# Attention sums from the value product itself, and another order of the second pass

## What is computed

```python
x = x + autocorrelation(layernorm(x), ctx, ctx)           # layer 0
x = x + lora_product(layernorm(x))
Q, K, V = layernorm(x) @ Wq + bq, ctx @ Wk + bk, ctx @ Wv + bv      # layer 1
scores = einsum('bhgqd,bhkd->bhgqk', Q, K) / sqrt(16)     # 8 key heads h, 4 query groups g
w = softmax(scores, axis=-1)
y = einsum('bhgqk,bhkd->bhgqd', w, V)
x = x + y @ Wo + bo
h = relu(layernorm(x) @ up_w) ** 2
shared = h @ down_w
routed = (layernorm(x) @ fc1 @ expert) * top2_sum(logits) @ fc2
x = x + layernorm(shared + routed, gamma, beta)
```

## Time and profile before

| | us |
|---|---|
| median of three runs | 686.14 (685.78 to 686.70) |
| profiled execution | 687.42 |
| its span | 685.6 |
| PE busy in the span | 654.6 (95%) |
| DVE, ACT, POOL busy | 511.4, 432.0, 378.5 |
| granted PE clock | 0.999 of 2.4 GHz |

### The profile page before, as it was taken

The page is one execution under the profiler, slowest core; times in us unless marked ns, Lnnn a source line. Parts: engine busy times, 40 slices in busy tenths (PEclk is TensorE's granted clock), DMA queues, the critical chain, the costliest instruction groups (busy, mean ns, idle before and its releaser), DMA issues.

```text
span 685.6 us, 12653 instructions
## 1 busy us (share of the span) xinstructions
PE 654.6 (95%) x3964; PEld 482.3 (70%) x3964; DVE 511.4 (75%) x1140; ACT 432.0 (63%) x793; POOL 378.5 (55%) x464
## 2 busy tenths in 40 slices
PE   7889999999999898999999999999999999998986
PEld 3455666666656476788778787887878878786775
DVE  4999998999975877777677677776777767775444
ACT  4788888888746785574655846658367474674221
POOL 1388999888775534435455354554454545535351
PEclk9999999999999999999999999999999999999999
DMA  8334434352126321121212312113021221211000
GB/s 269 121 109 124 139 123 124 123 180 98 62 94 173 117 79 33 46 64 61 63 35 57 90 33 61 45 49 90 31 61 54 69 61 31 61 31 47 17 16 31
DMA packets 32551, 54.37 MB, mean 79 GB/s; under 512 B 5344, under 2 KB 7136, under 8 KB 32512
## 3 DMA queue, kind: packets, MB, share of 16 engines
q1 hardware_dynamic: 32512, 53.90, 26.6%
HBM read 36.84 MB, written 8.39 MB: 66 GB/s over the span
## 4 chain that ended last, share of the span: by engine, by line
PE 78%; DVE 11%; issue 4%; DMA 3%; ACT 3%; POOL 1%; SPq 0%; POOLq 0%; DVEq 0%; ACTq 0%
PE ps_b L1295 8%; PE ps_b L1297 7%; PE ps_b L1296 7%; PE wide L1295 7%; PE wide L1297 6%; PE wide L1296 6%; PE ps_b L1496 4%; PE ps_a L1340 4%; PE bank L1432 3%; DMA ctx_t<-in_ctx 3%; PE wide L1422 3%; PE ps_b L1350 3%; PE ps_a L1295 2%; PE ps_a L1297 2%; PE wide L1550 2%
## 5 line engine op out<-in xcount | busy, mean ns | idle before, releaser
L780 POOL TENSOR_TENSOR va<-mv,small 128x1 f32<-128x1 f32 x80 | 15.3, 192 | 149.0 <-DVE mv L1274 79.5
L745 ACT ACTIVATE stage<-wide 128x512 f32<-128x512 f32 x30 | 16.3, 595 | 83.8 <-PE bank L1597 83.7
L868 POOL TENSOR_TENSOR y_l<-y,y_h 128x512 fp32r<-128x512 f32 x16 | 21.9, 1370 | 72.5 <-ACT y_h L653 72.5
L1142 DVE RECIPROCAL y<-ps_b 128x256 f32<-128x256 f32 x32 | 55.9, 1748 | 0.4 <-PE ps_b L1496 0.4
L676 ACT ACTIVATE probs<-wide 128x1024 f32<-128x1024 f32 x32 | 32.8, 1025 | 36.1 <-PE wide L1550 36.1
L1295 PE MATMUL wide<-up_h,t_h 128*128 128x512 f32 x128 | 52.1, 407 | 1.5 <-DVE t_l L1226 1.5
L1297 PE MATMUL wide<-up_h,t_l 128*128 128x512 f32 x128 | 50.9, 398 | 0.0
L1296 PE MATMUL wide<-up_l,t_h 128*128 128x512 f32 x128 | 50.4, 394 | 0.0
L1295 PE MATMUL ps_b<-down_h,ht_h 128*128 128x512 f32 x120 | 49.6, 413 | 0.4 <-DVE ht_l L1214 0.4
L782 POOL TENSOR_TENSOR rs<-va,small 128x1 f32<-128x1 f32 x80 | 44.5, 557 | 6.3
L1297 PE MATMUL ps_b<-down_h,ht_l 128*128 128x512 f32 x120 | 47.2, 393 | 0.0
(11 more groups left out here) (244 smaller groups left out, 2155.9 us busy)
## 6 DMA issues: line engine op xcount, KB each, us to landing
q_stack<-qt_h SPq DMA_DIRECT2D x128, 64.0 KB, 2.0
ctx_t<-in_ctx SPq DMA_DIRECT2D x16, 256.0 KB, 2.7
x_res<-in_x SPq DMA_DIRECT2D x16, 256.0 KB, 2.9
x_in<-x_rows SPq DMA_DIRECT2D x16, 256.0 KB, 2.7
ctx_t<-in_ctx_turned SPq DMA_DIRECT2D x16, 256.0 KB, 2.9
x_res<-x_rows SPq DMA_DIRECT2D x16, 256.0 KB, 2.9
out<-stage SPq DMA_DIRECT2D x15, 256.0 KB, 3.0
x_in<-in_x SPq DMA_DIRECT2D x8, 256.0 KB, 3.0
```

The lines of the kernel that those rows point to most:

```text
L1142: dve.reciprocal(y[:, :, b, :], part[:, 1]).then_inc(S["den_s"], 1)
```

## The change

One product gives numerators and sums. `vbd` is filled with ones at the start (before: zeros); the values of a head still overwrite its own 16 columns in its own 64 rows, so the 16 columns of the other head of the pair hold ones. `attend` now multiplies each head by itself: 64 rows of keys (one half of PE's rows) by 32 columns, 16 products a tile as before, each with half the rows. Bank 2 takes the first heads h = 0 of all pairs, bank 3 the second ones; in each group of 32 rows, 16 are the head's numerators and 16 its sums. `ones_bd` goes away, `place` (two columns that pick the first or the second 16 rows) comes instead.

The sums stand beside the numerators they belong to, 16 rows off. So ACT (`attended_out`) copies both banks to `sums[0]`, `sums[1]`, and bank 2 once more, scaled by `place[0]`, to `y`; four DMAs on SP's queue (`denominators`) and four on ACT's own move the sums by 16 rows into `den`, 32 KB each. DVE adds the second heads' numerators to `y` (`numerators`, a scalar_tensor_tensor), inverts `den` in two halves (`inverted`) and multiplies (`attended`, one product of the whole tile). `sums` lie in the memory of `x_h` and `x_l`, `den` in that of `y_h`.

`output` waits for `y_h` alone for its first eight matmuls and for `y_l` before the last four. PE's order, and with it ACT's, DVE's, POOL's and SP's, is another one: in `body2` the second half of the hidden layer is turned before `down(i, 0)`, the routed product's upper columns come after it, `down(i, 1)` and the norm's transposes come before `output`, and after `output` only `turned_maxima` stands before the lower columns of the routed product. PE waits for the exponentials (`attend_ready`) before `turned_hidden(i, 0)`.

```diff
 SP
+            def denominators(t):
+                if live(t):
+                    sp.wait_ge(S["sums_s"], 3 * t + 1)
+                    wait(sp, S["wo_ps"], t)
+                    for p in range(PAIRS):
+                        sp.dma_start(den[STACK * p:STACK * p + HD], sums[0][STACK * p + HD:STACK * (p + 1)]
+                                     ).then_inc(S["den_in"], 16)
             def body2(i):
                 load2(i + 4)
-                stacked(i + 3)
                 residual(i + 2)
+                denominators(i + 2)
...
+                stacked(i + 3)
 ACT
+            def attended_out(t):
+                if live(t):
+                    act.wait_ge(S["pv_ps"], 2 * t + 2)
+                    act.wait_ge(S["qy_ps"], capped(1, t + 2))
+                    for h in range(2):
+                        act.activation(sums[h][:].rearrange("p g b q -> p b g q"),
+                                       bank[2 + h].rearrange("p (b g q) -> p b g q", b=2, g=GROUPS), ACT.Copy
+                                       ).then_inc(S["sums_s"], 1)
+                    wait(act, S["wo_ps"], t)
+                    act.activation(y[:].rearrange("p g b q -> p b g q"),
+                                   bank[2].rearrange("p (b g q) -> p b g q", b=2, g=GROUPS), ACT.Copy, scale=place[0]
+                                   ).then_inc(S["sums_s"], 1)
+                    act.wait_ge(S["sums_s"], 3 * t + 2)
+                    for p in range(PAIRS):
+                        act.dma_start(den[STACK * p + HD:STACK * (p + 1)], sums[1][STACK * p:STACK * p + HD]
+                                      ).then_inc(S["den_in"], 16)
 ACT, body2
                     hidden_high(t, 0)
+                attended_out(i + 2)
...
                 context_high(i + 4)
                 keys_stacked(i + 3)
-                y_high(i + 2)
-                queries_stacked(i + 3)
...
                     hidden_high(t, 1)
...
+                queries_stacked(i + 3)
+                y_high(i + 2)
+                query_high(i + 4)
 DVE
+            def numerators(t):
+                    dve.wait_ge(S["sums_s"], 3 * t + 3)
+                    dve.scalar_tensor_tensor(y[:], sums[1][:], place[1], y[:], ALU.mult, ALU.add).then_inc(S["den_s"], 1)
+            def inverted(t, b):
+                    dve.wait_ge(S["den_in"], DEN_MOVES * (t + 1))
+                    dve.reciprocal(den[:, :, b, :], den[:, :, b, :]).then_inc(S["den_s"], 1)
             def attended(t):
...
+                    dve.wait_ge(S["den_s"], 3 * t + 3)
+                    dve.tensor_tensor(y[:], y[:], den[:], ALU.mult).then_inc(S["y_s"], 1)
 DVE, turn_two
                 queries_low(1)
-                attended(0)
+                numerators(0)
                 merged_low(0)
                 maxima(1, 0)
...
                 merged_low(2)
+                inverted(0, 0)
+                inverted(0, 1)
+                attended(0)
+                merged_low(3)
+                norm_low(2)
+                values(1)
                 third(0)
 DVE, body2
-                attended(i + 2)
+                numerators(i + 2)
                 if opening(i):
                     down_low(0)
+                context_low(i + 4)
+                normalised(i + 4)
+                maxima(i + 3, 0)
+                inverted(i + 2, 0)
+                t = i
+                if live(t) and not final(t):
+                    hidden_low(t, 1)
+                inverted(i + 2, 1)
+                attended(i + 2)
+                maxima(i + 3, 1)
...
-                third_norm(i + 2)
+                norm_low(i + 4)
                 values(i + 3)
-                keys_values(i + 4)
                 if opening(i):
                     down_low(1)
+                third(i + 2)
...
+                keys_biased(i + 4)
+                third_norm(i + 2)
                 queries(i + 4)
 PE
             def attend(t):
...
+                        for p in range(PAIRS):
+                            for h in range(2):
+                                k = slice(SEQ * h, SEQ * (h + 1))
+                                last = pe.matmul(bank[2 + h][STACK * p:STACK * (p + 1), HALF * b:HALF * (b + 1)],
+                                                 vbd[k, b, p].rearrange("k h d -> k (h d)"), probs[k, b, p, :],
+                                                 start=True, stop=True)
                         last.then_inc(S["pv_ps"], 1)
 PE, turn_two
                 scores(1, 0)
+                output(0)
+                products_kv(2)
                 queries(2)
                 scores(1, 1)
 PE, body2
                 turned_queries(i + 3)
+                attend_ready(i + 2)
...
                 rough_scores(i + 3, 0)
...
-                    wait(pe, S["y_s"], capped(2, t + 3))
+                    turned_hidden(t, 1)
+                    wait(pe, S["sums_s"], capped(3, t + 3))
                     down(t, 0)
...
+                t = i + 1
+                if live(t):
+                    routed_part(t, HALF, D + EXPERTS, bank[4])
                 rough_scores(i + 3, 1)
...
                     down(t, 1)
+                turned_norm(i + 4)
+                output(i + 2)
+                turned_maxima(i + 3)
+                t = i + 1
+                if live(t):
+                    wait(pe, S["x3_s"], capped(1, t + 2))
+                    routed_part(t, 0, HALF, bank[2][:, HALF:])
+                products_kv(i + 4)
```

More of the change, by code:

```diff
@@ L93, in constants @@
     small[:, HEAD0:HEAD0 + PART] = np.tile(np.repeat(np.eye(PART), HD, axis=0), (2, 1))
-    small[:, ONES0:ONES0 + 2 * HD] = np.kron(np.eye(2), np.ones((SEQ, HD)))
+    small[:, PLACE0:PLACE0 + 2] = np.tile(np.repeat(np.eye(2), HD, axis=0), (PAIRS, 1))
     for p in range(PAIRS):
@@ L135, in build @@
         head_of_pair = small[:, PAIR0 - FIRST:PAIR0 - FIRST + 2]
-        ones_bd = small[:, ONES0 - FIRST:ONES0 - FIRST + 2 * HD]
+        place = [small[:, PLACE0 - FIRST + h:PLACE0 - FIRST + h + 1] for h in range(2)]
         half, eps, minus = (small[:, c - FIRST:c - FIRST + 1] for c in (HALF0, EPS0, MINUS0))
@@ L157, in build @@
         x_in, ctx_t = sb("x_in", [P, D]), sb("ctx_t", [P, D])
+        with ExitStack() as tmp:
+            sums = [sb(f"sums{h}", [P, GROUPS, 2, SEQ], stack=tmp) for h in range(2)]
         x_h, x_l = sb("x_h", [P, D], F32R), sb("x_l", [P, D], F32R)
@@ L1243, in body2 @@
                     dve.tensor_tensor(rw[:], lg[:, 0:1], lg[:, 1:2], ALU.add).then_inc(S["rw_s"], 1)
-                maxima(i + 3, 0)
-                context_low(i + 4)
-                if isinstance(i, int) and i < 0:
-                    third(i + 2)
-                    normalised(i + 4)
-                else:
-                    normalised(i + 4)
-                    third(i + 2)
-                maxima(i + 3, 1)
-                t = i
-                if live(t) and not final(t):
-                    hidden_low(t, 1)
                 if closing(i):
@@ L1490, in attend @@
                     wait(pe, S["z_s"], t - 2)
+                    pe.wait_ge(S["probs_s"], 2 * t + 2)
+            def attend(t):
+                if live(t):
                     for b in range(2):
-                        pe.wait_ge(S["probs_s"], 2 * t + b + 1)
-                        for n in range(2):
-                            for p in range(PAIRS):
-                                lhs = ones_bd if n else vbd[:, b, p].rearrange("k h d -> k (h d)")
-                                last = pe.matmul(bank[2 + b][32 * p:32 * (p + 1), 256 * n:256 * (n + 1)], lhs,
-                                                 probs[:, b, p, :], start=True, stop=True)
+                        for p in range(PAIRS):
[4 more added lines that the diff above has]
+                                                 start=True, stop=True)
                         last.then_inc(S["pv_ps"], 1)
@@ L1594, in turned_hidden @@
                 if not final(t):
+                    wait(pe, S["ht_lo"], 2 * t + part)
                     wait(pe, S["qx_lo"], capped(1, t + 4))
@@ L1640, in body2 @@
                 if live(t) and not final(t):
-                    wait(pe, S["y_s"], capped(2, t + 3))
+                    turned_hidden(t, 1)
+                    wait(pe, S["sums_s"], capped(3, t + 3))
                     down(t, 0)
-                output(i + 2)
-                t = i
-                if live(t) and not final(t):
-                    turned_hidden(t, 1)
-                rough_scores(i + 3, 1)
                 t = i + 1
                 if live(t):
-                    wait(pe, S["x3_s"], capped(1, t + 2))
-                    routed_part(t, 0, HALF, bank[2][:, HALF:])
-                if opening(i):
-                    turned_maxima(2)
-                    keys_values(3)
-                else:
-                    keys_values(i + 4)
-                    turned_maxima(i + 3)
+                    routed_part(t, HALF, D + EXPERTS, bank[4])
+                rough_scores(i + 3, 1)
```

71 lines of the change are left out of this document (35 added, 36 removed).

## The result

The changed kernel takes **716.09 us** (median of four runs, 715.10 to 718.75) against 686.0 of the kernel before; the ratio is 1.0443, 95% interval 1.0414 to 1.0472. Its profiled execution took 715.77 us, with a span of 713.9 against 685.6. The forecast was 714, its range 691 to 726.

A forecast was written before the change was run, and what follows sets the result against it. PE was taken to bound the twelve full turns, the order itself the opening turns. With the change, +17.2 us in the full turns and +10.3 in the opening put 686.14 at 713.6, say 714 us; range 691 to 726.

The forecast's parts named there:

- Attend, 0.87: PE's attend, 1.86 us a turn, gets shorter by 0.87 (between 0 and 0.93) with matmuls on half the rows.
- The wait moved up, 0.1: PE waits for the second exponentials before the hidden layer's four transposes: 0.1 us a turn, at most 0.5.
- the wait uncovered, 0.59: After output only turned_maxima covers the lower routed product's wait for x3: PE waits 0.59 us every turn.
- An issue on ACT, 0.62: Each of ACT's four DMA issues takes 0.62 us of ACT's time, from similar copies on SP.
- rival 1: An issue on ACT costs a whole tile's 0.39 us; a turn lasts 28.6, the kernel 702 us; chance 0.18.
- rival 2: ACT's queue lets go at once, PE does not wait; a turn takes 27.89, the kernel 692 us; chance 0.13.
- rival 3: SP and ACT slow each other's issues to twice 0.62 us; a turn lasts 32.0, the kernel 746; chance 0.07.
- The chain to the low half: 15.8, a turn of 29.5, +17.2: Behind ACT's issues, DVE's low half comes at 15.8 us, down(i, 1) waits 1.6; turn 29.5, twelve turns +17.2.
- The opening, +10.3: Turn two and turn -1 lengthen: +3.9 for the series, +2.5 for y, +3.9 in turn -1; together +10.3 us.
- The end, 0 within 2: The last three turns pay the x3 wait in full, 0.95, against attend's 0.87 each: 0, within 2 us.
- The sum: +17.2 and +10.3 make +27.5 us on the median 686.14: 713.6, say 714 us; chance 0.50.
- Rivals 4 and 5: 4: new order packs turn two and turn -1, 678 us, chance 0.08. 5: gains and waits cancel, 686 us, 0.04.

The follow-up runs named there:

- the fifth run: Changed kernel with all eight sum copies issued on SP, PE turning the next norm behind output and DVE doing norm_low behind third: 701.18 us.
- run 1: Changed kernel with ACT's four DMA issues moved behind SP's four, nothing else moved: 697.76 us.
- run 8: Changed kernel with ACT's four issues placed behind the copies of x3 and of the context in every turn of `body2`: 699.45 us.
- run 3: Changed kernel with each of ACT's four copies sent in two halves, eight issues for the same bytes: 781.39 us.
- run 2: Changed kernel with DVE making the second low half of the hidden layer ahead of the first reciprocal, issues still on ACT: 718.60 us.
- run 4: Changed kernel with 36 idle products of 512 columns, which nobody reads, filling PE's gaps in turn two and turn -1: 713.54 us.
- Run 7: Run 6 with turn -1's down-weight splits moved, 6 idle products there for 20, and output ahead of down(i, 1) in the last turn with an output: 686.40 us.
- run 6: The fifth run with idle products in turn two and turn -1, and steps in both reordered on PE, DVE and ACT: 689.07 us.

## Why the prediction held, point by point

**Attend, 0.87.** Measured 0.84. 32 products on half the rows take 1.02 us where 32 on all rows took 1.86. That PE can start them nearly twice as fast no row of before had shown; the forecast took it from pairs of products on row halves.

**The wait moved up, 0.1, and the wait uncovered, 0.59.** Measured 0.31 by the step, and 0.59. The first was put 0.2 too low: the overlap of two matmuls that is lost at a wait was not in it. It also accounts for the full turns of the fifth run: 28.09 - 0.84 + 0.31 = 27.56, measured 27.57. In the kernel after it costs nothing, since PE waits for the low half anyway. The fifth run shows that the second was a matter of place: with the turned norm behind output instead of ahead of it, it is gone. The prediction had said that nothing hides it; that holds for the change as it was made.

**An issue on ACT, 0.62.** This was the number that told the forecast from rivals 1 to 3. The middle one of the 64 is 611 ns, on SP at the same time 590 (least, middle and most, ns):

```profile
L680 ACTq DMA_DIRECT2D den<-sums x64: 519/611/1277, 225.2 to 666.8; - x64
```
```profile
L480 SPq DMA_DIRECT2D den<-sums x64: 507/590/1526, 224.7 to 666.4; - x64
```

So rival 1 (0.39), rival 2 (at once) and rival 3 (1.24) are out, and taking the row of the same kind of transfer was right. The dispatch of some 50 ns of the Trainium skill, "DMA: Bandwidth & Descriptors", section "Anatomy of one DMA — SWDGE (gpsimd) path", is stated for GpSimd's path; an issue on ACT's and SP's queues takes twelve times as long here, so it could not be carried over to them. The sequencer's time, which the Trainium skill, same page, section "Issuing engines are not separate DMA queues", calls usually small beside the DMA itself, is here 0.61 us beside the 2.0 us from an issue to its landing, and four in a row, 2.45 us, take longer than one landing.

**The chain to the low half: 15.8, a turn of 29.5, +17.2.** Measured 15.5 and 29.25, +14.0. Three terms were a little too long: the context was there at 8.06 and not at 8.15, the reciprocal's step is 1.66 and not 1.78 (from 471.72 to 473.38; the second one, whose result the next row reads, has a step of 1.76, from 473.93 to 475.69), the low half took 0.62 and not 0.68. Together that is 0.27; the steps from the context's copy to normalised were 0.05 longer than summed, and the terms add up to 15.74, which the forecast rounded up to 15.8. That makes 0.27 a turn, 3.2 in twelve: the difference. The chain itself was shown: it goes when the issues leave ACT (run 1) and when they stand behind the context's copy (run 8), it grows with their number (run 3), and it comes out in y when the low half is put ahead (run 2). DVE's numerators took 1.61 us, not 0.7, but still ended before the context came.

**The opening, +10.3.** Measured +13.3. Turn -1 came out as forecast, 3.9. Turn two came out at 9.4 where 3.9 for the series and 2.5 for y, 6.4, had been summed. The missing term is the clock: output(0) took 5.3 us instead of the 2.8 that the sum had, 2.5 of the 3.0. The scores ahead of it were slow too (1.20 for 0.72), but output stood 0.63 for y behind them, so that cost nothing; y itself came 0.35 later than allowed (output starts 20.82 into the turn, the sum had 20.47). That PE's idle times could cost PE's speed as well stood nowhere in the sum. The kernel before also has an order of its own for turn -1 (third ahead of normalised on DVE, turned_maxima ahead of keys_values on PE), which the change drops; what that alone costs was not measured. In turn -1 the right number had a partly wrong reason: of the named waits y's came (3.67), x3's did not (0.34), and the slow output took its place until run 4 brought it back (2.12).

**The end, 0 within 2.** Measured +2.7, just outside. In the last turn with an output the lower routed product waits 0.78 for x3 and the next norm's turn 1.45 for the normalised x3; down(i, 1) had stood behind output there as cover and now stands ahead of it. Run 7 put it back and won 0.4 only, because y was then the last to be ready. But 1.5 of the 2.7 is a fall of the clock in this execution, and not the order: in the turn from 659.59 attend takes 1.89 us (661.78 to 663.67) at a granted clock near 0.50.

```profile
661.00:663.00 2.00, 2.00 (x28) 1.12 (x35) 1.17 (x2) 0.66 (x2) 2.00 (x2) 0.51 0.00 0
```

The turn lasts 24.99; in run 4, where every engine has the same program there, the clock is 1.00 until the turn ends, attend takes 1.03, and the turn lasts 23.44 (in that execution the fall comes behind it, 0.72 from 684 to 690). In run 8 the clock there is 0.99, as before, and all that follows the twelve full turns takes 78.4 us for 77.2 before: +1.2, inside the forecast.

**The sum.** The forecast was 2 us off in the median and 0.8 in the span (27.5 for 28.3), and so near because terms cancelled: +3.2 too much in the full turns, 3.0 too little in turn two, 2.7 too little at the end, and a start 1.7 earlier. That is luck in the number; the chain in the full turns, which decides, is not. Rivals 4 and 5 fell: the new order did not pack the opening, it lengthened it.

**What stays open.** How the 12 us between runs 5 and 6 part into clock and order was not measured, nor why the clock falls at one place of the end in one execution and at another or nowhere in the next, with nearly the same idle times before.

## What to carry to other kernels

A DMA's issue is work of the engine that issues it, here 0.6 us each for 16 partitions or 8 (a whole tile's took 0.36): count the issues as instructions in that engine's program, follow what is queued behind them, and put them behind the copies that others wait for. A chain that comes late has several ends, and moving one of them ahead shows the next, so shorten its front. Twelve full turns won 6 us once the side effects were gone and two turns of the opening lost it again: stretches that run once need a sum of their own, with the clock in it: a product of output took 0.43 us at 0.50 and 0.233 at 1.00.

## What the hardware did that was not expected

- TensorE's granted clock halved inside the kernel. In turn two PE had idled 1.96, 2.52 and 2.71 us with short stretches of work between; after that the records show 0.50 from 238 to 245 and products at 0.43 us a step, and 1.00 again in the stretch from 249.00. In run 3 the same came in a full turn, and at the end of the profiled execution of after behind waits of 1.1 us and less. Idle time on PE was thus paid twice. Idle products kept the clock for both outputs in run 4, but not from 235 to 238 nor behind the wait of 2.12; in run 6, with another order besides, it was 1.00 in both turns.
- ACT's sequencer starts a DMA's issue while copies ahead of it in the program have not started (run 8). The Trainium skill, "Perfetto Trace Analysis", section "DVE / Act Engine Instruction (TENSOR_ADD, Activation, etc)", has the sequencer free for its next instruction once one is pushed into the wait queue; the rows of run 8 agree.
- DVE's numerators, one pass with both operands in SBUF, take 1.61 us in a full turn and 0.75 in turn two and turn -1; normalised 1.51, and 0.54 in turn two. That POOL's work beside them makes the difference was not tested.
